# Attention and the next pair's projection emitted at 2:1 instead of 1:1 in an eight-core transformer layer

## What is computed

```python
xn = layernorm(x)
q, k, v = xn @ wq.T, xn @ wk.T, xn @ wv.T            # 16 heads of 64
q_mag, k_mag = softplus(q), softplus(k)
# each head's 64 values become 128: times cos and times sin of position * frequency
q_embed = interleave(q_mag * cos(qp), q_mag * sin(qp))
k_embed = interleave(k_mag * cos(kp), k_mag * sin(kp))   # kp = qp + a bias per head
attn = softmax(q_embed @ k_embed.T / 8)
x + (attn @ v) @ wo.T + ffn(xn)                      # ffn: 3 cycles of a coupling net
```

## Time and profile before

| | us |
|---|---|
| median of 2 runs | 4217.63 (4216.8 to 4218.46) |
| profiled execution, its own time | 4229.15 |
| its span on the slowest core (core 7), first to last instruction | 4227.2 |
| spans of the eight cores | 4192.9 to 4227.2 |
| mean granted TensorE clock of the cores, as a share of full speed | 0.782 to 0.793 |

### The profile page before, as it was taken

How to read it: one execution, slowest core, us unless ns; L and a number is a source line. 1 busy time by engine, 2 the same in 40 slices (tenths; PEclk the granted TensorE clock), 3 DMA queues, 4 the chain that set the end, 5 groups by cost and what they waited for, 6 DMA issues and landing times.

```text
span 4227.2 us, 35770 instructions; the slowest of 8 cores (4192.9 to 4227.2 us)
## 1 busy us (share of the span) xinstructions
PE 2681.5 (63%) x10486; PEld 1090.2 (26%) x10486; DVE 1446.4 (34%) x2435; ACT 1647.1 (39%) x2082; POOL 0.2 (0%) x4
## 2 busy tenths in 40 slices
PE   0432676776677866675642566777767785676664
PEld 0211232222232213332321222322222221332322
DVE  5434322333322323333336433223333142333333
ACT  2101565665567102221213355666556701222221
POOL 0000000000000000000000000000000000000000
PEclk9855899888898557787875788998889956777766
DMA  5422000110000030211215010001100003022121
GB/s 150 143 93 63 24 14 13 26 26 24 17 13 16 11 122 30 85 65 46 89 54 167 23 26 24 14 14 26 25 24 17 5 12 105 30 90 70 40 80 55
DMA packets 84372, 208.45 MB, mean 49 GB/s; under 512 B 25559, under 2 KB 26584, under 8 KB 84184
## 3 DMA queue, kind: packets, MB, share of 16 engines
q1 hardware_dynamic: 84184, 206.16, 16.0%
HBM read 134.27 MB, written 41.94 MB: 42 GB/s over the span
## 4 chain that ended last, share of the span: by engine, by line
PE 45%; DVE 22%; DMA 14%; issue 11%; ACT 5%; SPq 2%; DVEq 1%; ACTq 0%
PE ps_w L170 23%; PE ps_s L170 14%; PE ps_pv L170 8%; DVE stream L170 6%; DMA xt<-x 3%; ACT pt L170 3%; DMA tmp<-qmag 3%; DMA xt<-ffn_s 2%; DVE vp L170 2%; DVE qh L170 2%; DVE ke L170 2%; DMA xt<-cnw 2%; SPq L170 2%; DMA ke<-kmag 1%; DVE tmp L170 1%
## 5 line engine op out<-in xcount | busy, mean ns | idle before, releaser
L170 ACT ACTIVATE pt<-ps_s,cpool 128x1024 bf16<-128x1024 f32 x1024 | 1087.1, 1116 | 877.7 <-PE ps_s L170 873.9
L170 PE MATMUL ps_pv<-pt,vp 128*65 128x512 bf16 x2048 | 663.7, 408 | 289.3 <-DVE tmpB L170 228.7
L170 PE MATMUL ps_s<-qh,ke 128*128 128x512 bf16 x2048 | 663.9, 408 | 103.1 <-ACT pt L170 80.1
L170 PEld LDWEIGHTS ps_pv<-pt,vp 128*65 128x65 bf16 x2048 | 235.8, 118 | 571.8 <-issue 381.9
L170 PEld LDWEIGHTS ps_s<-qh,ke 128*128 128x128 bf16 x2048 | 174.0, 103 | 474.4 <-issue 397.4
L170 ACT ACTIVATE h<-ps_w,b1f 128x512 bf16<-128x512 f32 x192 | 132.3, 689 | 415.5 <-PE ps_w L170 415.5
L170 PE MATMUL ps_w<-ofm,w1t 128*128 128x512 bf16 x1024 | 263.0, 422 | 10.5 <-ACT ofm L170 10.5
L170 ACT CAST ofm<-ps_w 128x128 bf16<-128x128 f32 x256 | 49.9, 281 | 446.0 <-PE ps_w L170 445.9
L170 PE MATMUL ps_w<-ident,sbf 128*128 128x128 bf16 x512 | 64.7, 306 | 247.7 <-DVE sbf L170 247.7
L170 DVE COPY rowstg<-ps_pv 1x1024 f32<-1x1024 f32 x32 | 39.1, 1222 | 451.6 <-PE ps_pv L170 451.4
L170 PE MATMUL ps_w<-h,w2t 128*128 128x512 bf16 x768 | 180.0, 393 | 0.0
(11 more groups left out here) (110 smaller groups left out, 2522.1 us busy)
## 6 DMA issues: line engine op xcount, KB each, us to landing
xt<-x SPq DMA_DIRECT2D x128, 512.0 KB, 4.0
ffn_s<-xt SPq DMA_DIRECT2D x32, 512.0 KB, 2.6
xt<-ffn_s SPq DMA_DIRECT2D x32, 512.0 KB, 3.9
out<-stream SPq DMA_DIRECT2D x32, 512.0 KB, 2.9
ke<-kmag SPq DMA_DIRECT2D x32, 256.0 KB, 3.4
qh<-qmag SPq DMA_DIRECT2D x32, 256.0 KB, 3.9
tmp<-qmag SPq DMA_DIRECT2D x32, 256.0 KB, 3.8
xt<-cnw SPq DMA_DIRECT2D x16, 512.0 KB, 3.9
```

The lines of the kernel that those rows point to most:

```text
L170: inst = getattr(engine, op.method)(*op.args, **op.kwargs)
```

## The change

One number: `drive` takes two attention steps for every projection step.

```diff
         for j in range(NP):
             ga = gen_attention(j)
             gp = gen_projembed(j + 1) if j + 1 < NP else iter(())
-            drive((ga, 1), (gp, 1))
+            drive((ga, 2), (gp, 1))
```

## The result

The changed kernel is slower: the ratio of its time to the kernel before is 1.036 (95% interval 1.033 to 1.039). With 4218.1 us for the kernel before, the median of its ten runs, that is about 4369 us. In some executions the cores of one die, sometimes of both, run at a lower clock, whatever the kernel; the figures here are of undisturbed executions, or of the undisturbed die where only four cores are named.

A forecast was written before the change was run, and what follows sets the result against it. No engine full: PE paces projection rounds, ACT softplus and lone attention, PE and DVE alternate in v chunks. Per boundary 26.5 us removed, 42.1 added, net 15.6; times 14, less 2, gives 216 us: about 4434 us, range 4390 to 4475.

The forecast's parts named there:

- slow matmuls: PE at the lower clock level after waits: two stretches go, 3.4 us saved; 3.0 us added on resuming, per boundary.
- readout waits: PE waiting for four readouts per pair, 19.9 us before; three at 1.5 us remain, 15.3 us saved.
- the two tails: Pair boundary: PE idle before the next scores, 23.8 us added; then before the first `ps_pv` matmul, 11.3 us added.
- the hole of 14.46: PE idle before 647.64: a `ps_pv` matmul waits for a readout behind the whole embedding on DVE; 14.46 us, to go.
- the lone steps: 28 attention steps without projection, at ACT's 1.01 us against PE's 0.86; none left in a projecting pair, 4.1 us saved.
- Rival 2: One tail only: the new pair's first `ps_pv` waits 1.5 us instead of 11.3; 81 us slower, 4299 us; chance 4%.
- Rival 1: Interleaving wins: embedding still hidden at the boundary, -17.3 us each, -242 in all, 3976 us; chance 3%.
- The weights: At the boundary PE waits for the next `wqt` load, issued behind the readout's DMAs; 1.0 us added.
- softplus: Exp and Ln hold ACT, now with two exponentials between, so PE's score matmuls wait longer for `pt`; 3.0 us added.
- Rival 3: The clock stays down: rounds 2 to 9 after the holes run at the lower level; 4710 us, half 4570; chance 5%.

The follow-up runs named there:

- a_head1: Changed kernel (2:1) with head 1's embedding emitted in the next pair, behind the last readout, qmag and kmag kept twice; 4276.6 us, a single execution.
- b_delay: Kernel before (1:1) with head 1's embedding held back until attention has emitted 50 steps; 4055.0 and 4065.3 us.
- b_fill3: Kernel before (1:1) with three extra 512-column matmuls behind each transpose, results not read; 4163.5, 4166.4 and 4184.5 us, ratio 0.988.
- a_fill3: Changed kernel (2:1) with three extra 512-column matmuls behind each transpose; 4350.4, 4352.3 and 4354.4 us, ratio 1.031 to the kernel before.
- a_hoist: Changed kernel (2:1) with the three DMAs of head 0's embedding issued before the last v chunk; 4254.8, 4263.4 and 4289.1 us, ratio 1.011 to the kernel before.

## Why the prediction was wrong, and what in it was right

The step that failed is the term "slow matmuls". It was put at 3.4 us removed and 3.0 added per boundary, and at no change for the v chunks. The runs showed that the v chunks lose 4.3 us a period to the lower clock level before and 2.4 after, and that PE resumes at the lower level with the first weights in only 6 of 12 periods. The rest of this section works that out.

**By stretch.** For each part of a period I take what it lasts beyond PE's 512-column matmuls at 0.216 us each, the rate of a gapless round (2.59 us for 12); means of 12 periods. The forecast's terms are sorted into the same parts, readout waits going where the readouts went. A row moves by up to 0.5 us with the exact matmul at which the parts are cut.

| part of the period | before | after | change | forecast |
|---|---|---|---|---|
| q chunks | 1.7 | 0.7 | -1.0 | +0.2 |
| both softplus, k chunks | 8.1 | 12.4 | +4.2 | +4.5 |
| v chunks 0 to 2 | 15.0 | 13.9 | -1.1 | +1.5 |
| last v chunk to the next pair's weights | 28.7 | 37.8 | +9.1 | +9.4 |
| sum | 53.5 | 64.8 | +11.2 | +15.6 |

(The periods themselves give 10.9.)

**Right: the two tails.** Their lengths of 23.8 and 13.7 us were read from the kernel before and came as 23.78 and 13.75. The whole part from the last v chunk on was forecast at +9.4 and measured at +9.1, with the removal of the hole of 14.46, of the lone steps and of one slow stretch already in it. Rival 2, one tail only, falls with the hole of 8.99 us and with a_head1: the second tail has a price of its own. Rival 1, interleaving wins, needed cover for the embedding, and the 19.45 us of idle PE show that there was none. In b_delay, at 1:1, a gain came from where the cover stands; no run tried it at 2:1. The weights were forecast at 1.0 us and cost 0.9 on the mean. The estimate beside it, that the load would be there in time, did not come: the wait stood in all 12 periods, 0.6 to 1.6 us.

**Right in sum, not in shape: softplus.** Forecast +3.0. The stretches with the softplus lengthened by about 2.7 (the table's 4.2 less the 1.5 of a readout that moved into them). The waits that the trace books to `pt` did not grow as said, 5.7 to 5.3 us a period, where 8 to 9 had been named as the mark: in half of the pairs the clock falls in the first wait of 2.17, as at 858.80, and the matmuls behind it run at half rate and fill what would have been the second wait.

**Wrong: the term "slow matmuls".** It removed 3.4 us for two stretches, added 3.0 on resuming, and took for granted that the slow matmuls among the transposes of the v chunks stay as they are. (The first of its two stretches was placed loosely, too: behind the last transposes, at 612.01, PE is at the upper level; it slows at 616.7, behind the readout wait of 2.36.) The slow matmuls of the v chunks did not stay as they were. Counted as time lost to the lower level, the v chunks cost 4.3 us a period before, in 2.3 stretches, and 2.4 after, in 1.3 stretches. At 1:1 a chunk of the v part holds one attention step between transposes and projection matmuls; at 2:1 it holds two, PE is busy for 27.64 of 36.42 us instead of 22.78 of 32.08, and the granted clock is 0.91 instead of 0.84. That makes 1.9 of the 2.6 us missing in that row of the table, the third readout at 0.88 instead of 1.5 most of the rest. The pair b_fill3 and a_fill3 shows the cause by taking it away: with the clock full in the v chunks of both kernels, 2.2 us of the missing time come back there. In the q chunks another 1.2 us is missing: the earlier trace rows had shown PE still at the lower level with the first weights, and I took that for every pair, but it is so in 6 of 12. Rival 3, the clock stays down, did not come: from 697.82 on the rounds take 2.59 us. Over a period the change made the granted clock worse (0.85), by the holes at the boundary, and inside the v chunks it made it better.

**Also missed: the ends.** 7 x 10.9 is 76 us an item, but the attention stretches of the two items grew by 70 each (means of eight cores). At an item's first pair two attention steps instead of one fit into the wait for the first weights (on core 7 PE waits 3.7 us instead of 6.2 in the first item, and not at all instead of 3.0 in the second). Fewer lone steps behind the last pair's projection may be the rest; that was not taken apart. I had put 1 us per item on this, it was about 6. Together, 14 x 4.7 + 2 x 5 = 76 us would be missing by the profiles, against 65 by the runs. That difference I leave open; the two profiled executions lie 11 us above and 8 us below the times that the ratio gives.

**The range.** It held the scatter of "slow matmuls" at -3 to +2 per boundary, for the resumption alone. That the clock inside the v chunks would move had no place in it, and neither had the ends. With the forecast 65 us too high, a range of 44 us downwards was too narrow.

## What to carry to other kernels

Before a ratio between two interleaved streams is changed, find the serial piece at the end of the shorter one (here an embedding of 18 to 24 us on DVE with DMA flights in it) and ask what stands beside it afterwards: a ratio that empties one stream earlier lays that piece bare, once per boundary. Ask where a long block stands in the order of its engine, relative to the small operation that another engine waits for: moving it behind that readout gave 160 us, changing the ratio cost 151. And treat the clock as a result of the order: a stretch in which PE takes turns with another engine may gain or lose its full clock by a change that doesn't touch it.

## What the runs showed of the hardware

- Three matmuls of 512 columns whose result nobody reads, set in PE's idle time behind each transpose, made the kernel before faster, ratio 0.988 (0.983 to 0.993), with the granted clock of the v chunks raised from 0.84 to 1.00. One such matmul in the same place left the clock there at 0.85 to 0.95 and attention 2 to 6 us shorter. The same three at 2:1 gained no more than 0.5%.
- A cast on DVE from PSUM to SBUF took 226 ns for 128x64 elements and 426 ns for 128x256, as group means. From these two, 1.04 ns per element of a row and 159 ns per instruction; eight small casts last 1.8 us, two large ones 0.85. The Trainium skill, page "VectorE: DVE Perf Modes", section "The TRN2 errata — SBUF-src ops pay a fixed extra latency per instruction", gives 120 cycles plus one per element for such a copy at 0.96 GHz. As an estimate by that page that is 192 and 392 ns: the slope agrees, and the fixed part is 34 ns short by both rows.
- With PE busy for 27 to 29 of 33 us on all eight cores, the granted clock was 1.00, the level of 2.4 GHz, on each of them for these 33 us (539.90 to 573.00).
- The DMAs between partition halves of head 0's embedding kept DVE idle for 3.06 and 4.56 us in the bare tail, and not at all when they were issued before the last v chunk (a_hoist). What looked like a chain on DVE was to one third DMA flight, 7.6 of 23.8 us.
